# An identity matrix stored to DRAM and read back, in place of a select on GpSimd, in a graph attention layer

## What is computed

```python
h = jnp.maximum(_layernorm(x, axis=-1), 0.0)
H = h @ W_fc + b_fc
s_src = H @ w_att[:d]
s_dst = H @ w_att[d:]
scores = s_src[:, None] + s_dst[None, :] + b_att
scores = jnp.where(A > 0, scores, jnp.float32(NEG_INF))
alpha = jax.nn.softmax(scores, axis=1)
return x + alpha @ H
```

## Time and profile before

| | |
|---|---|
| median of 3 runs | 210.57 us (207.68 to 211.06) |
| profiled execution | 207.97 us |
| its span, first instruction to last | 206.2 us |
| PE, PEld, DVE, ACT, POOL busy | 74%, 70%, 70%, 33%, 1% |
| instructions | 3218 |
| HBM read, written | 69.34 MB, 2.10 MB |

### The profile page before, as it was taken

How to read it: one execution, slowest core, us unless ns; L and a number is a source line. 1 busy time by engine, 2 the same in 40 slices (tenths; PEclk the granted TensorE clock), 3 DMA queues, 4 the chain that set the end, 5 groups by cost and what they waited for, 6 DMA issues and landing times.

```text
span 206.2 us, 3218 instructions
## 1 busy us (share of the span) xinstructions
PE 152.5 (74%) x1130; PEld 144.1 (70%) x1130; DVE 144.5 (70%) x446; ACT 69.0 (33%) x157; POOL 1.7 (1%) x10
## 2 busy tenths in 40 slices
PE   0058973946695599999767988875999997689940
PEld 0026962846694599989766988765999986688930
DVE  2415999992643969999644557788689967358992
ACT  2206655670662145432430222222522234502100
POOL 1010000000000000000000000000000000000000
PEclk9999999696999999999999999998799999999995
DMA  6999991715286699999999999999999999999821
GB/s 175 397 420 437 378 415 43 246 65 191 114 317 198 248 409 415 428 445 421 432 424 429 420 429 426 429 421 428 434 417 434 424 413 442 429 415 399 344 99 54
DMA packets 7940, 71.67 MB, mean 348 GB/s; under 512 B 881, under 2 KB 1650, under 8 KB 3314
## 3 DMA queue, kind: packets, MB, share of 16 engines
q1 hardware_dynamic: 7344, 71.18, 84.2%
q10 hardware_dynamic: 578, 0.26, 0.5%
HBM read 69.34 MB, written 2.10 MB: 346 GB/s over the span
## 4 chain that ended last, share of the span: by engine, by line
DMA 43%; DVE 23%; PE 16%; issue 10%; ACT 4%; POOL 0%; DVEq 0%; POOLq 0%; ACTq 0%
DMA ring<-adj 43%; PE bank L867 11%; DVE mask L497 9%; DVE features L518 2%; DVE x_sb L618 2%; ACT weighted L372 2%; PE bank L848 2%; DVE stats L512 2%; DVE weighted L704 1%; ACT relu_T L362 1%; PE bank L837 1%; DVE high_bits L590 1%; PE bank L827 1%; DVE features L593 1%; ACT relu L383 1%
## 5 line engine op out<-in xcount | busy, mean ns | idle before, releaser
L867 PE MATMUL bank<-features,mask 128*128 128x258 f32 x1024 | 135.9, 292 | 26.4 <-DVE mask L497 22.9
L867 PEld LDWEIGHTS bank<-features,mask 128*128 128x128 f32 x1024 | 129.8, 196 | 31.8 <-DVE mask L497 27.2
L497 DVE TENSOR_SCALAR mask<-ring 128x1536 fp32r<-128x1536 int32 (+3 forms) x70 | 65.9, 957 | 29.6 <-DMA ring<-adj 24.8
L442 ACT ACTIVATE mask<-ring,half_steep 128x512 fp32r<-128x512 int32 x39 | 26.1, 716 | 68.4 <-DMA ring<-adj 68.4
L618 DVE SCALAR_TENSOR_TENSOR x_sb<-sums,inv_den,x_sb 128x128 f32<-128x128 f32 x56 | 17.3, 347 | 0.6
L455 ACT COPY sums<-bank 128x258 f32<-128x258 f32 x28 | 10.5, 374 | 14.1 <-PE bank L867 12.1
L848 PE MATMUL bank<-w_sb,relu_T 128*128 128x128 f32 x64 | 10.0, 303 | 6.3 <-ACT relu_T L362 6.3
L848 PEld LDWEIGHTS bank<-w_sb,relu_T 128*128 128x128 f32 x64 | 8.7, 211 | 7.6 <-ACT relu_T L362 7.6
L372 ACT ACTIVATE weighted<-bank,w_over_std 128x128 f32<-128x128 f32 x32 | 9.2, 368 | 9.2 <-PE bank L848 7.5
L383 ACT ACTIVATE relu<-x_sb,neg_mean 128x128 f32<-128x128 f32 x32 | 9.8, 390 | 4.9 <-DVE neg_mean L527 4.9
L822 PE MATMUL bank<-w_T_and_a,a_wide 128*128 128x128 f32 x2 | 0.8, 488 | 12.9 <-POOL a_wide L347 12.9
(11 more groups left out here) (72 smaller groups left out, 46.3 us busy)
## 6 DMA issues: line engine op xcount, KB each, us to landing
ring<-adj SPq DMA_DIRECT2D x16, 1792.0 KB, 13.4
ring<-adj SPq DMA_DIRECT2D x11, 2048.0 KB, 17.1
ring<-adj SPq DMA_DIRECT2D x7, 1536.0 KB, 8.0
ring<-adj SPq DMA_DIRECT2D x2, 768.0 KB, 6.9
x_sb<-x SPq DMA_DIRECT2D x1, 1024.0 KB, 13.6
ring<-adj SPq DMA_DIRECT2D x1, 1024.0 KB, 15.6
ring<-adj SPq DMA_DIRECT2D x4, 256.0 KB, 15.9
out<-x_sb SPq DMA_DIRECT2D x2, 448.0 KB, 10.0
```

The lines of the kernel that those rows point to most:

```text
L442: nc.scalar.activation(mask[:, n % MASKS, cols - SHARE:cols], ring[:, n // 2 % RING, end - SHARE:end], ACT.Sigmoid, bias=half_steep[:], sc ...
L497: nc.vector.tensor_scalar(mask[:, n % MASKS, 0:cols], ring[:, n // 2 % RING, begin:begin + cols], 0.0, None, ALU.is_gt).then_inc(masks_rea ...
L867: last = nc.tensor.matmul(bank[:, BANKS[g][b], 0:WIDE], mask[:, n % MASKS, at:at + P], features[:, t, :, :].rearrange("p h d -> p (h d)"), ...
```

## The change

The tensor one_and_zeros (128 partitions of 129 elements) is cleared on POOL, and its first column set to one. ACT stores it to a DRAM tensor of 128 x 129 elements, waits until it has landed, and loads the first 128 x 128 of these as 128 rows of 128. A one stands in DRAM at every 129th element, so that row p of the load has it in column p. turn(0) waits for this load. The affine_select goes away; ident is written by the load only.

```diff
+        one_and_zeros = sb("one_and_zeros", [P, P + 1], F32)
...
+        ident_scratch = nc.dram_tensor("ident_scratch", [P * (P + 1)], F32)
...
-        constants_ready = sem("constants_ready")
+        one_and_zeros_ready = sem("one_and_zeros_ready")
+        ident_stored = sem("ident_stored")
+        ident_landed = sem("ident_landed")
...
         def _(pool):
-            nc.gpsimd.memset(ident[:], 0.0).then_inc(cleared, 1)
+            nc.gpsimd.memset(one_and_zeros[:], 0.0).then_inc(cleared, 1)
             nc.gpsimd.memset(ones_row[:], 1.0).then_inc(ones_ready, 1)
             pool.wait_ge(cleared, 1)
-            nc.gpsimd.affine_select(out=ident[:], in_=ident[:], compare_op=ALU.not_equal, fill=1.0, base=0,
-                                    pattern=[[-1, P]], channel_multiplier=1).then_inc(constants_ready, 1)
+            nc.gpsimd.memset(one_and_zeros[:, 0:1], 1.0).then_inc(one_and_zeros_ready, 1)
             nc.gpsimd.memset(half_steep[:], -0.5 * STEEP).then_inc(half_steep_ready, 1)
...
             act.dma_start(w_sb[:], w_fc).then_inc(w_landed, 16)
+
+            act.wait_ge(one_and_zeros_ready, 1)
+            act.dma_start(ident_scratch.ap().rearrange("(p d) -> p d", d=D + 1), one_and_zeros[:]).then_inc(ident_stored, 16)
+            act.wait_ge(ident_stored, 16)
+            act.dma_start(ident[:], ident_scratch.ap()[0:P * P].rearrange("(p d) -> p d", d=P)).then_inc(ident_landed, 16)
...
                 pe.wait_ge(relu_ready, PER * c + PER)
                 if c == 0:
-                    pe.wait_ge(constants_ready, 1)
+                    pe.wait_ge(ident_landed, 16)
```

## The result

| | before | changed |
|---|---|---|
| median | 209.18 us (4 runs, 207.68 to 211.06) | 212.91 us (4 runs, 211.94 to 213.7) |
| profiled execution | 207.97 us | 212.92 us |
| its span | 206.2 us | 211.0 us |

The ratio is 1.0208, with a 95% interval of 1.0115 to 1.03: slower, but whether by more than 2% is left open. A larger sample of both kernels, beside the experiments, gave 210.51 us against 210.09 (10 and 24 executions, ratio 1.0046, 0.9986 to 1.0106), which is no difference clear of the spread. With a piece of filling work that takes this spread out of both kernels, the change costs 1.7 us.

A forecast was written before the change was run, and what follows sets the result against it. Bound in three stages: first loads, compute, then the adjacency stream, with turn(0) setting the middle stage's start. Identity lands at 16.4 us, so turn(0) starts 0.8 us later, the rest hidden: 210.57 + 0.8 = 211.4 us, range 208.0 to 214.7.

The forecast's parts named there:

- turn(0) sets the start, and the identity's landing sets turn(0): Start of the kernel: first transposes wait for the identity, starting at 16.45 instead of 15.64 us, +0.8 us.
- The idle before the select is the select's: POOL's start: 10.99 us of idle goes with the select; any cost falling to the last reduction is hidden.
- rival C: POOL's start: idle belongs to the third instruction, identity lands at 19 to 22.6 us; +5, 215.6 us; chance 0.04.
- The store, 2.13 to 11.2: ACT's queue at the start: store issued at 2.13 us behind w_sb, landing at 11.2, between 10.25 and 13.15.
- The load, 5.2 us: ACT's queue behind the store: load takes 5.2 us, the middle of 3.4 and 6.9; identity lands at 16.4.
- the upper row: Upper bound for the identity's load at the start: 6.9 us, the time w_sb took.
- The lower row: Lower bound for the identity's load at the start: 3.4 us, w_T_and_a's time when engines were half full.
- What waits behind ACT: Table load, relus and v_rows behind ACT's wait: v_rows at 14.6 us against 14.47, hidden by the identity's wait.
- rival E: PE's start: the clock rises later, at most 2.1 us behind 23.70 us; +2.9 in all, 213.5 us; chance 0.06.
- A: Start: both transfers near their lower ends, turn(0) at 13.7, 1.9 us earlier; 208.6 us; chance 0.20.
- B: Start: both transfers near their upper ends, identity at 20.05, turn(0) 4.5 us later; 215.1 us; chance 0.16.
- D: Start: small transfers take 1.6 us each despite other traffic, turn(0) at 7.5, 8.1 us earlier; 202.5 us; chance 0.06.

The follow-up runs named there:

- e4: Changed kernel with ACT's transfers reordered: the store ahead of line and w_sb, w_sb behind the identity's load; 209.05 us, ratio 0.9987 to the kernel before.
- e9: Changed kernel with SP's larger loads (x's third stage, the ring's later pairs) held back until the identity has landed; 206.54 us, ratio 0.987 to the kernel before.
- e3: Kernel before with POOL's copy of a_wide moved ahead of its wait and select, which is kept; 209.17 us, ratio 1.0006.
- e5: Changed kernel once more, unaltered, for the spread of its executions; 210.51 us over 10 executions (209.83 to 213.43).
- e1: Changed kernel with 36 extra small products on PE, read by nobody, between units 6 and 7 of group 0; 212.1 us.
- e6: Changed kernel with 14 extra small products on PE, read by nobody, between units 6 and 7 of group 0; 208.71 us.
- e7: Kernel before with 14 extra small products on PE, read by nobody, between units 6 and 7 of group 0; 207.01 us, ratio 0.9927.
- e8: Kernel before with the select kept, but a_wide copied by ACT and no longer by POOL; 207.41 us, ratio 0.9879 (0.972 to 1.0038).
- e10: Kernel before with the select kept, a_wide copied by ACT, and 14 extra products on PE between units 6 and 7; 203.88 us, ratio 0.9801.

## Why the prediction was right, and where not

- *turn(0) sets the start, and the identity's landing sets turn(0).* Right. Nine profiles bear it out. The kernel before has turn(0) at 15.6 us. With turn(0) at 12.6 (twice) or 15.5 the mask of unit 1 lies 3.0 or 0.1 us ahead of its own, at 15.7 level, and at 15.9, 17.3, 17.4, 17.6 and 18.8 it lies 0.2, 1.7, 1.8, 2.0 and 3.2 us behind. In e4 and e9 something else takes over: w_sb, and the ring's loads.
- *The idle before the select is the select's.* Right, by the changed profile and by e3; rival C falls. The last reduction, which might now pay for it, had 166.38 us of cover; it began 0.1 us behind its data in either kernel, so whatever it had to pay was hidden, as costed.
- *The store, 2.13 to 11.2.* It landed at 10.68 (and 10.07 in e5): taken 0.5 us too long. That w_sb's place ahead of it matters fits e4, where the store took 4.7 us without it, issued 1.0 us earlier. One of my signs of being wrong was a transfer of over 8 us; the store took 8.53 and met it, but so did the forecast itself, with 9.1 us, so the sign was badly set.
- *The load, 5.2 us.* It took 6.73 (7.14 in e5, 7.68 in e1). This is the mis-sized term, by 1.5 us. I took the middle of 3.4 and 6.9 because nothing of its own queue was ahead of it, and that argument failed: in e9, with the same store and the same queue ahead of it, the load took 1.69 us once SP's loads were away. What it pays for is the other queue's traffic. The stretch had a DMA share of 1.01 to 1.05, fuller than the one w_sb was slow in, so the upper row was the near one. The lower row was misread besides: the 0.54 of 0 to 4 us is a mean over 1.7 us without a packet and 2.3 us at 0.94, so w_T_and_a's 3.4 us were no price of half-full engines. Together +0.8 forecast, +1.9 in the profile, 1.7 between e6 and e7.
- *What waits behind ACT.* Right: table load and relus behind the wait, v_rows done at 13.9 against the 14.6 forecast, all hidden by the load. How near it stood shows in e9, where the load took 1.69 us and these relus set turn(0).
- *The clock.* I looked for its effect where it rises, at 23.7 us, and priced rival E at 2.1 us there. The place was wrong. The rise does move: the first twelve mask products took 2.92 us before, 2.19 in the changed kernel, 2.88 in e5 and 1.70 in e7, but e7's mask of unit 4 came only 0.1 us earlier for it (28.76 for 28.88). So a moving rise, which I had named as a sign of being wrong, came about and cost next to nothing. What costs time is the wait between units 6 and 7, near whose end the clock falls. How long the low stretch behind lasts differs between executions: 3.4 us in three profiles (before, e4, e5), 10.2 in e9, 13.6 to 13.7 in three (changed, e3, e8), some 3 us of time, with and without the change. The clue was in the times shown, 207.68 beside 210.57 and 211.06, which I took as noise.
- *The number.* 211.4 came out as 212.91, inside the range, but the 3.7 us between the two medians are not the 0.8 forecast. About 1.7 of them are the change. The rest fits the longer low stretch: the profiled execution of the changed kernel had it, and the other three (211.94 to 213.7) took about as long, while six of its ten further executions (e5) took 209.83 to 210.55; that those three had it too is likely and not shown. So the number was in part luck: I forecast against a median, 210.57, that was itself one of the longer executions, and the longer ones of the changed kernel came to meet it. Like against like, profile with short stretch against profile with short stretch, the forecast was 208.8 and 209.83 came. The 2% of the first sample is more than the change costs: 1.7 us in 207 is 0.8%, which is also where I had put most of the chance (0.84 for within 2%).
- *Rivals.* A fell (turn(0) at 17.4, 17.6 and, with the filling, 17.3 and 18.8 in the profiles of the changed kernel, never at 13.7), B was nearer on the load alone, D fell: the quickest 64 KB transfers beside SP's loads took 3.4 us (w_T_and_a) and 4.7 us (e4's store). The Trainium skill (DMA: Bandwidth & Descriptors, Anatomy of one DMA) gives the figure named with D for transfers issued through GpSimd, while these are issued by ACT; my estimate from it, some 2.2 us for 64 KB, is near e9's 1.69 us and the 1.6 and 2.1 us of the last stores, where the engines had little else to do, and far from every 64 KB transfer beside SP's loads.
- *A reading.* The DMA row is near full again from slice 14 on (counted from 0, as my slices 1 to 5 were), not 16, and rises to 8 tenths once in between. Nothing in the sum hangs on it.

What stays open: why the low stretch is sometimes short and sometimes long. That filling the wait ends it is shown; what decides its length isn't. And whether the select's idle would be as long without the stream of loads beside it was not tried.

## What to carry to other kernels

Work that a stalled engine holds up behind it in program order may matter more than the stalled instruction: moving one 0.4 us copy to an idle engine gained 3.1 us (e10 against e7), and replacing the select by two transfers lost 1.7 (e6 against e7), though it freed that copy as well. Price a small transfer by the traffic of all queues at the moment it is issued, not by its bytes: the same 64 KB took 1.7, 6.7 and 8.4 us here. And when the executions of one kernel differ by more than the effect looked for, look for a stretch of low clock behind a wait of PE before reading a difference of medians as an effect.

## What the runs showed of the hardware

- A read of 64 KB from DRAM took 1.69 us on emptying engines (e9) and 6.73 to 8.4 beside a stream that kept the DMA share near 1.0. Where the 6.73 us of the changed kernel went is in its DMA queues (queue: packets, MB, share of the engines), first for 10.7 to 13.7 us, the load issued at 10.70, then for 14 to 16.5 us; q1 is SP's, q10 ACT's:

```profile
q1 hardware_dynamic: 109, 1.26, 98.5%
```

```profile
q1 hardware_dynamic: 132, 1.02, 96.4%
q10 hardware_dynamic: 122, 0.06, 8.2%
```

  In the first stretch ACT's queue has no packet at all; in the second it has nearly as many as SP's, but SP's carry 1.02 MB and these 0.06. The load's first packet came 3.4 us after its issue and its last 2.9 us later, 0.4 us before the landing. In e9 the first came 0.9 us after the issue and the last 0.4 us later. So the traffic of the other queue cost some 2.5 us ahead of the first packet and as much between the packets.
- 14 small products (about 3.2 us of work) in a wait of PE kept the clock at the upper level behind it: e7's median of 207.01 us lies 0.9 us under the best and 3.1 us under the median of the 24 executions of the kernel before.
- The select's idle was 10.38 us (e3), 10.99 (kernel before), 11.16 (e8) and, in the chain, 10.96 (e10), whether the copy stood ahead of it, behind it or on another engine. The Trainium skill (GPSIMD Engine Reference, 2.1 Instruction dispatch) has about 6 us for the first call of a freshly loaded kernel. This idle is nearly twice as long, beside a full stream of loads; that it is the load of which that page speaks fits its being nameless and the select's alone, and no run here shows it.
